# A feed-forward layer with routed experts, twice around an attention layer: both passes sort in two parts, the late chain stands among the shared tiles, and the routing weights are applied at the mix

## The chip, the cores and the metric

One core of one Trainium2 chip runs the whole program in one launch. The metric is the device time of an execution in microseconds (us); several executions give a median.

## The reference, cut to what matters

```python
def ffn(x):                       # x: (2, 1024, 128); 7 routed experts, top 2, HID = 352
    out = expert(x, sg, su, sd)   # silu(h @ g.T) * (h @ u.T) @ d.T, the shared expert
    probs = softmax(x @ wr.T + rb)
    scores, idx = top_k(probs, 2);  scores = scores / scores.sum(-1)
    w = sum(scores[..., None] * one_hot(idx, 7), axis=-2)
    for e in range(7):
        out = out + w[..., e:e+1] * expert(x, rg[e], ru[e], rd[e])
    return out

x = x + 0.5 * ffn(layernorm(x))
x = x + attention(layernorm(x))   # 16 heads of 8, causal, sequence 1024, batch 2
x = x + 0.5 * ffn(layernorm(x))   # same weights
```

## The kernel before, in words

2048 tokens are 16 tiles of 128 (TT), or 4 chunks of 512 (NCH). Everything is fp32, and each product is made of three fp32r products of high and low halves; so every operand is split on its way, the high half by ACT (a cast) and the low one by DVE (a subtraction). The passes of the feed-forward layer are f = 0 and f = 1.

*Sorting.* Of each token the router (`router_dve`, L510, a chain of 15 small DVE operations and one exp on ACT) finds two experts. `places_pe` (L575) counts with two matmuls, `places_dve` (L631) makes from the counts the row of each (token, choice), and `experts_dve` (L655) which expert each of the NJ = 38 routed tiles has. Then POOL sorts: `sort_pool` (L923) is one indirect DMA that writes 128 rows of 132 numbers (weight, id, 128 values, id, weight) into `z_rows` in DRAM, 32 of them in a pass (L928). As the last tile of an expert isn't full, `z_rows` is blanked before (`blank_sp`, L1038), pass 0's 2.6 MB and pass 1's 9.1 MB, on SP's queue at the start. SP loads the sorted tiles back to `zg` in ten batches (`rows_load_sp`, L960; 2 tiles, then 4 each): pass 0 in one DMA per batch, pass 1, where each expert has a fixed region of rows, one per tile from an address in a register. Pass 0 sorts all tokens in one part (PARTS); pass 1 sorts chunks 0 and 1 and then 2 and 3, but its tiles are listed once, after both.

*The tiles' loop.* `ffn_pe`, `ffn_act` and `ffn_dve` (L769, L819, L907) go through the same steps, one job each: 13 (pass 0) or 14 (pass 1) shared tiles, the 38 routed tiles, the other shared tiles (BEFORE, JOBS, L76). A job is 6 matmuls for gate and up (L707 to L709), silu on ACT (L799), the product on DVE (L840; for a routed tile times the weight of the row, L843), 3 transposes (L723), high and low half (L807, L849), 6 matmuls down (L733, L736), and the way out on DVE: two adds to `x` for a shared tile (L888, L890), one reduction to the ring `ys` of 8 for a routed one (L884), from where POOL scatters it to `y_rows` (`scatter_pool`, L932). Step `BEFORE + j - 2` transposes the batch that begins with routed tile j (L756; `batch_at`). In pass 0 the first 8 steps also carry a weight group each (transposes on PE, halves on ACT and DVE; 24 groups in all, TP_FIRST = 16 of them ahead of the loop). At the end SP loads the two rows of each token back, chunk by chunk, and `mix_dve` (L895) adds them to x (L904).

*Order by hand.* Each engine's list is written out in `build` (L1765). Pass 0: norm and logits of all four chunks, router, places, experts, weights, `ffn`. Pass 1: during the last group of heads the chain of chunks 0 and 1 runs (projection, norm, logits, router); after it TAIL_PE, TAIL_ACT, TAIL_DVE (L1720) do the same for chunks 2 and 3 before `ffn_pe(K, 1)` begins. POOL does all sorts, then all scatters, in order. SP's queue: inputs, blank of pass 0, constants of the attention, blanks of pass 1, sorted tiles, clears of `keys` (L1117, 12 DMAs of 512 KB), loads for the mix, attention.

Of the kernel before, what the change touches and what calls it, by code (L numbers as in the profile page):

```python
# [69 lines left out]
assert sum(n for _, n in BATCHES) == NJ  # L70
# [22 lines left out]
def at_bank(q):  # L93
    return AT_BANKS[q % 2]
# [12 lines left out]
ROW = 2 + EMB + 2  # L107
W_COLS, ID_COLS = (0, ROW - 2), (1, ROW - 1)
# [87 lines left out]
def loads(p, u, d):  # L196
# [12 lines left out]
TP_GROUPS = [("g", 0), ("u", 0), ("g", 1), ("u", 1), ("d", 0), ("d", 1)] + \  # L209
            [(w, x) for x in range(2, EXPERTS) for w in ("g", "u", "d")]  # L210
NTP = len(TP_GROUPS)
TP_FIRST = 16
# [4 lines left out]
PM_BANK = [EARLY_BANKS[0], EARLY_BANKS[1], 3, 4]  # L217
LATE_N_BANK = [EARLY_BANKS[2], EARLY_BANKS[1], 5, 3]
R_BANKS = [[R_BANK], [EARLY_BANKS[0], R_BANK]]
# [4 lines left out]
N_CONST2 = 8  # L224
N_SPARES = 4
N_GIVEN = 4
# [9 lines left out]
def place_memory(K, ctx):  # L236
# [8 lines left out]
    K.z_dram = [K.nc.dram_tensor(f"z_rows{f}", (SORTED[f], ROW), F32, kind="Internal").ap() for f in range(2)]  # L245
# [23 lines left out]
    K.rank_i = sb("rank_i", [P, NGATE], mybir.dt.int32)  # L269
    K.stats = sb("stats", [P, 2, TPC, 6])  # L270
# [3 lines left out]
    K.rstd = sb("rstd", [P, 2, TPC])  # L274
    K.z0 = sb("z0", [P, TPC, EMB])
# [3 lines left out]
    K.ids = sb("ids", [P, 2, TT])  # L279
    K.again = {SPAN: sb("again", [P, NGATE, SPAN]), TT: sb("again_half", [P, NGATE, TT])}  # L280
# [3 lines left out]
    K.d_run = sb("d_run", [P, NGATE * SPAN])  # L284
    K.d_cnt = sb("d_cnt", [P, 7, NGATE])
    K.to_row = sb("to_row", [P, NJ], mybir.dt.int32)
    K.slots = sb("slots", [P, SPAN], mybir.dt.int32)
    K.w_row = sb("w_row", [P, NJ])
    K.id_row = sb("id_row", [P, NJ])
    K.w_at = sb("w_at", [P, NJ], mybir.dt.int32)  # L290
    with ExitStack() as s:
        zt = [sb(f"zt_{part}", [P, TOKENS], F32R, scope=s) for part in ("h", "l")]
        with ExitStack() as s2:
# [25 lines left out]
            with ExitStack() as s3:  # L319
# [6 lines left out]
                with ExitStack() as s4:  # L326
# [12 lines left out]
                    K.d_pos = sb("d_pos", [P, NGATE * SPAN], scope=s4)  # L339
                    K.d_slot = sb("d_slot", [P, SPAN], scope=s4)  # L340
# [9 lines left out]
    zrows = [[rows[:, c * TPC:(c + 1) * TPC, 2:2 + EMB] for c in range(NCH)] for rows in K.zrow]  # L350
# [31 lines left out]
    K.z_sc, K.spares, K.given = sem("z_sc"), sem("spares"), sem("given")  # L382
# [5 lines left out]
    K.consts2 = sem("consts2")  # L388
    K.A = {n: sem(f"a_{n}") for n in
# [36 lines left out]
def norm_rstd_pool(K, k, c):  # L426
    e, v = K.nc.gpsimd, c % 2
    e.wait_ge(K.NS[k]["mv"], c + 1)
    e.tensor_scalar(K.var_e[:, v, :], K.mv[:, v, :, 1], LN_EPS, None, ALU.add).then_inc(K.NS[k]["rstd"], 1)
    e.wait_ge(K.NS[k]["rstd"], 2 * c + 1)  # L430
    e.tensor_tensor(K.rstd[:, v, :], K.var_e[:, v, :], K.half_neg[:, :], ALU.pow).then_inc(K.NS[k]["rstd"], 1)


def norm_z_dve(K, k, c):
    e, v = K.nc.vector, c % 2
    e.wait_ge(K.NS[k]["rstd"], 2 * c + 2)
    e.wait_ge(K.NS[k]["mv"], c + 1)
    if c > 1 and k == 1:
        e.wait_ge(K.NS[k]["tr"], c - 1)
# [28 lines left out]
def part_of(f, c):  # L468

    return next(h for h, (t0, t1) in enumerate(PARTS[f]) if t0 <= c * TPC < t1)  # L470


def logits_pe(K, f, k, c):

    e = K.nc.tensor
    if f == 0 and c == 0:
        e.wait_ge(K.sw_lo, 5)
    e.wait_ge(K.NS[k]["lo"], c + 1)
    if f == 1 and c == 0:
        e.wait_ge(K.A["xup"], 2)  # L480
    for t in range(c * TPC, (c + 1) * TPC):
# [20 lines left out]

def chosen(K, f, h):

    t0, t1 = PARTS[f][h]
    flat = K.r_sel[:, 2 * t0 * NGATE:2 * t1 * NGATE]
    return flat.rearrange("p (r t e) -> p r t e", r=2, e=NGATE)


def router_dve(K, f, h):  # L510
    e, s, (t0, t1) = K.nc.vector, K.RS, PARTS[f][h]
    n, ts = t1 - t0, slice(t0, t1)
    r_log, r_exp, r_c, r_w = (v[:, ts, :] for v in (K.r_log, K.r_exp, K.r_c, K.r_w))
# [5 lines left out]
    if f == 0:  # L519
        e.wait_ge(K.ld["bias"], 16 * N_BIAS)  # L520
# [1422 lines left out]
```

## Time and profile before

| what | us |
|---|---|
| median of 3 runs (lowest to highest) | 751.13 (746.61 to 751.75) |
| the profiled execution, its own time | 749.79 |
| its span, first to last instruction | 747.8 |
| PE busy | 608.3 (81%) |
| DVE busy | 479.6 (64%) |
| ACT busy | 311.4 (42%) |
| POOL busy | 210.0 (28%) |
| mean granted clock of PE | 0.895 of full speed |

The trace is of one execution; its own time stands 2.0 us over its span and 1.3 under the median. PE, DVE, ACT, POOL and SP are the engines (TensorE, VectorE, ScalarE, GpSimd, SyncE); PEld is PE's weight load, which overlaps its matmuls. A busy share is a mean over stages that have different limits, so stages are read one at a time. L12 is line 12 of the kernel.

### The profile page before, as it was taken

How to read it: one execution, taken by the hardware profiler on the slowest of the kernel's cores; microseconds unless marked ns; L12 is line 12 of the kernel's file. 1: busy time of each engine (PE TensorE's matmuls, PEld its weight loads, DVE VectorE, ACT ScalarE, POOL GpSimd, SP SyncE). 2: the span in 40 equal slices, each digit the busy share in tenths (PEclk: the TensorE clock that was granted, in tenths of full speed). 3: DMA queues.
4: the chain of work that ended last, by engine and by line, in shares of the span. 5: the costliest groups of instructions: out<-in, count | busy, mean ns of one | idle time of the engine just before them, and what ended most of it. 6: DMA issues, size and time to landing. Idle time of an engine off the chain costs nothing.

```text
span 747.8 us, 12989 instructions
## 1 busy us (share of the span) xinstructions
PE 608.3 (81%) x3900; PEld 453.4 (61%) x3900; DVE 479.6 (64%) x1178; ACT 311.4 (42%) x628; POOL 210.0 (28%) x284
## 2 busy tenths in 40 slices
PE   3642799999837789999999999999977539999990
PEld 3531788999736445555555555554556438999980
DVE  8730566666684796777777776775456326766663
ACT  2230334444314106566665656566751013344440
POOL 5177003444333101111121112111226730244440
PEclk9985799999956799999999999999985559999996
DMA  9996695000246502112020202000001123101006
GB/s 225 320 370 244 167 211 123 27 31 30 66 120 211 193 3 57 37 24 59 3 58 0 58 0 58 1 1 4 1 2 38 51 62 88 34 25 33 29 29 172
DMA packets 44657, 61.03 MB, mean 82 GB/s; under 512 B 5495, under 2 KB 35198, under 8 KB 43582
## 3 DMA queue, kind: packets, MB, share of 16 engines
q1 hardware_dynamic: 39104, 50.72, 24.3%
q0 software_dynamic: 4480, 9.25, 3.7%
q8 instruction: 29, 0.48, 0.3%
q10 hardware_dynamic: 1022, 0.40, 0.3%
q14 instruction: 22, 0.18, 0.1%
HBM read 29.79 MB, written 30.30 MB: 80 GB/s over the span
## 4 chain that ended last, share of the span: by engine, by line
PE 67%; DVE 9%; issue 6%; another core or an unknown queue 5%; DMA 4%; ACT 3%; POOL 2%; SPq 1%; POOLq 0%; DVEq 0%; ACTq 0%
PE psum L1348 11%; PE psum L1370 10%; PE psum L1305 10%; PE psum L733 6%; PE psum L707 5%; PE psum L709 4%; PE psum L708 4%; PE psum L723 4%; PE psum L736 4%; DVE mxp L1422 3%; PE psum L1310 2%; DMA yc<-y_rows 2%; PE psum L756 2%; ACT probs L1482 1%
## 5 line engine op out<-in xcount | busy, mean ns | idle before, releaser
L1422 DVE TENSOR_REDUCE mxp<-psum 128x4 f32<-128x512 f32 x288 | 184.3, 685 | 58.7 <-PE psum L1305 33.0
L1482 ACT ACTIVATE probs<-psum 128x512 f32<-128x512 f32 (+1 forms) x304 | 164.4, 586 | 120.7 <-PE psum L1348 117.3
L1348 PE MATMUL psum<-queries,keys 128*128 128x512 f32 (+3 forms) x384 | 133.2, 395 | 0.5 <-ACT probs L1482 0.2
L1305 PE MATMUL psum<-keys,queries 128*128 128x512 f32 (+3 forms) x384 | 128.2, 381 | 5.1 <-DMA queries<-q_stack 3.0
L935 POOL DMA_INDIRECT y_rows<-ys,to_row x76 | 72.8, 958 | 176.6 <-DVE ys L884 173.8
L799 ACT ACTIVATE silu<-psum 128x352 f32<-128x352 f32 x108 | 50.1, 464 | 142.9 <-PE psum L709 111.0
L1533 POOL TENSOR_SCALAR_AFFINE_SELECT probs<-probs 128x512 f32<-128x512 f32 x64 | 40.6, 635 | 210.4 <-ACT probs L1482 210.4
L1305 PEld LDWEIGHTS psum<-keys,queries 128*128 128x128 f32 x384 | 70.4, 195 | 41.1 <-DVE mxp L1422 32.9
L1348 PEld LDWEIGHTS psum<-queries,keys 128*128 128x128 f32 x384 | 65.6, 190 | 42.6 <-ACT probs L1482 38.1
L733 PE MATMUL psum<-wall,at_h 128*128 (+1 forms) x324 | 69.4, 325 | 21.1 <-DVEq L892 17.8
L1370 PE MATMUL psum<-probs,vg 128*32 128x512 f32 (+3 forms) x768 | 81.8, 498 | 4.8 <-POOL probs L1533 4.8
L723 PE MATMUL psum<-ident,act 128*128 128x128 f32 x324 | 56.3, 285 | 28.6 <-issue 28.3
L843 DVE SCALAR_TENSOR_TENSOR act<-silu,w_row,psum 128x352 f32<-128x352 f32 x76 | 44.1, 581 | 44.2 <-ACT silu L799 33.1
L849 DVE TENSOR_TENSOR at_l<-psum,at_h 128x384 fp32r<-128x384 f32 x108 | 59.6, 552 | 18.3 <-issue 11.6
L733 PEld LDWEIGHTS psum<-wall,at_h 128*128 128x128 f32 x324 | 48.8, 199 | 27.8 <-issue 15.2
L723 PEld LDWEIGHTS psum<-ident,act 128*128 128x128 f32 x324 | 43.4, 146 | 33.1 <-issue 30.3
L807 ACT CAST at_h<-psum 128x384 fp32r<-128x384 f32 x108 | 51.3, 475 | 25.6 <-PE psum L723 11.4
L707 PE MATMUL psum<-wall,zs_h 128*128 x152 | 54.1, 356 | 3.3 <-DVE zs_l L871 3.3
L736 PE MATMUL psum<-wall,at_l 128*128 (+1 forms) x324 | 50.2, 265 | 0.0
L709 PE MATMUL psum<-wall,zs_l 128*128 x152 | 49.4, 325 | 0.0
L708 PE MATMUL psum<-wall,zs_h 128*128 x152 | 49.3, 324 | 0.0
L736 PEld LDWEIGHTS psum<-wall,at_l 128*128 128x128 f32 x324 | 47.8, 199 | 0.0
(221 smaller groups left out, 881.2 us busy)
## 6 DMA issues: line engine op xcount, KB each, us to landing
z_rows<-zg SPq DMA_DIRECT2D x4, 2508.0 KB, 14.1
keys<-q_stack SPq DMA_DIRECT2D x12, 512.0 KB
yc<-y_rows SPq DMA_DIRECT2D x16, 256.0 KB, 3.5
keys<-k_stack SPq DMA_DIRECT2D x32, 128.0 KB, 4.3
queries<-q_stack SPq DMA_DIRECT2D x8, 512.0 KB, 4.2
zg<-z_rows SPq DMA_DIRECT2D x38, 66.0 KB, 1.8
zg<-z_rows SPq DMA_DIRECT2D x9, 264.0 KB, 4.7
k_stack<-zt_h SPq DMA_DIRECT2D x8, 256.0 KB, 3.1
```

What stands on the lines that cost most here:

```text
L707: e.matmul(dst, zh, weight(K, base, hi, HID), start=True, stop=False)
L708: e.matmul(dst, zh, weight(K, base, lo, HID), start=False, stop=False)
L709: ins = e.matmul(dst, zl, weight(K, base, hi, HID), start=False, stop=True)
L723: ins = e.transpose(bank(K, at_bank(q))[:, k * P:(k + 1) * P], K.act[:, q % 2, k * P:(k + 1) * P], K.ident[:, :])
L733: e.matmul(dst[:, 0:2 * EMB], K.at_h[:, q % 2, k * P:(k + 1) * P], weight(K, base, DN + 2 * k * EMB, 2 * EMB), start=(k == 0), stop=False, ...
L736: ins = e.matmul(dst[:, 0:EMB], K.at_l[:, q % 2, k * P:(k + 1) * P], weight(K, base, DN + 2 * k * EMB, EMB), start=False, stop=(k == 2), s ...
L935: e.indirect_dma_start(K.y_dram[f], bass.IndirectOffsetOnAxis(ap=K.to_row[:, j:j + 1], axis=0), K.ys[:, j % RING_Y, :], None).then_inc(K.y ...
L1305: ins = e.matmul(dst[:, at0 * P:(at0 + nb) * P], K.queries[u][:, i * P:(i + 1) * P], K.keys[u][:, j, k0 * P:(k0 + nb) * P], start=(m == 0) ...
L1348: ins = e.matmul(slot(K, u, d, n)[:, m * (q1 - q0):(m + 1) * (q1 - q0)], K.keys[v][:, j, kt * P:(kt + 1) * P], K.queries[v][:, q0:q1], sta ...
L1370: ins = e.matmul(bank(K, O_BANK[half])[32 * j:32 * j + 32, q0 - half * CHUNK:CHUNK], K.vg[:, kt, j, :], K.probs[:, kt % 2, j, q0:q1], star ...
L1422: e.tensor_reduce(K.mxp[:, j, 4 * b:4 * b + 4], bank(K, r_bank).rearrange("p (m k) -> p m k", k=P), AX.X, ALU.max).then_inc(K.A["taken"], 1)
L1482: e.activation(K.probs[:, kt % 2, heads[0]:heads[-1] + 1, q0:q1], src, ACT.Exp, scale=SCALE).then_inc(K.A["ex"], 1)
```

## The change

- Both passes sort in two parts (chunks 0 and 1, chunks 2 and 3), into fixed regions of REGION = 2176 rows per expert. No region is blanked in pass 0: seven more indirect DMAs (`pads_pool`) write 128 rows of zeros behind each expert's last row, and only six tiles at the end (EXTRA) are blanked. Pass 1's rows (8.3 MB, now 130 numbers each) are blanked behind pass 0's loads and the clears.
- The list of routed tiles has two parts (`lists_dve`): ten tiles (WHOLE) that part 0 alone fills, in whole tiles, then the other 28. SP loads each list when its part is sorted, in both passes one DMA per tile.
- Behind every indirect DMA of a sort and of the first ten scatters POOL clears 384 numbers of `idle` (`pause_pool`).
- The row carries id and a code of the first choice, no weight. DVE finds from the code whether a row is a first or second choice (`rows_ids_dve`); the weights are kept in `K.w` and applied in `mix_dve`, one 128x128 operation per tile and choice.
- The normalised values come from ACT (`norm_z_act`), except for chunks 0 and 1 of the last norm; POOL makes two more small operations per chunk for it.
- Pass 0: only 11 weight groups stand ahead of the loop; part 1's router, places and both lists stand in its steps 0 to 5. Pass 1: the late chain of chunks 2 and 3 stands in steps 0 to 11 of the loop.
- A shared tile's and expert's weights are read from a static place, not through a register. `act` is transposed into one bank, not two, until step 13 or 16.

```diff
+HALF = TT // 2
+PARTS = [(0, HALF), (HALF, TT)]
+WHOLE = -(-(SEQ * 2 - ROUTED * (P - 1)) // P)
+LISTS = [(0, WHOLE), (WHOLE, NJ - WHOLE)]
+REGION = TOKENS + P
...
-TP_FIRST = 16
+TP_FIRST = 11
...
+def norm_z_act(K, k, c):
+    e, v = K.nc.scalar, c % 2
+    e.wait_ge(K.NS[k]["rstd"], 4 * c + 4)
...
+    for t in range(TPC):
+        ins = e.activation(K.z[k][c][:, t, :], K.x[:, c * TPC + t, :], ACT.Identity, bias=K.mr_neg[:, v, t:t + 1],
+                           scale=K.rstd[:, v, t:t + 1])
+    ins.then_inc(K.NS[k]["z"], 1)
...
+def lists_dve(K, f, h):
...
+    e.tensor_tensor(ends, tile0.unsqueeze(2).to_broadcast(wide), cnt(K, ENDS, ROUTED).unsqueeze(1).to_broadcast(wide),
+                    ALU.is_ge).then_inc(s["at"], 1)
+    e.wait_ge(s["at"], routed(f, h, "at", 1))
+    e.tensor_reduce(raw[:, 0, :], ends, AX.X, ALU.add).then_inc(s["at"], 1)
...
@@ act_tr_pe
     if q >= 2:
-        e.wait_ge(s["lo"], q - 1)
-    if q == 1:
-        e.wait_ge(K.RS["slot"], routed(f, len(PARTS[f]) - 1, "slot", 1))
+        e.wait_ge(s["lo"], q - 1 if q > ONE_AT[f] else q)
+    elif q:
+        e.wait_ge(s["lo"], q)
...
@@ ffn_pe
+        for what, c in (FRONT_PE if f == 0 else TAIL_PE).get(step, ()):
+            late_pe(K, f, what, c)
...
@@ act_dve
-    kind, n = JOBS[f][q]
-    if kind == "s":
-        e.tensor_tensor(act, silu, up, ALU.mult).then_inc(s["act"], 1)
-    else:
-        e.wait_ge(s["ids"], 3 * BATCH_OF[n] + 3)
-        e.scalar_tensor_tensor(act, silu, K.w_row[:, n:n + 1], up, ALU.mult, ALU.mult).then_inc(s["act"], 1)
+    e.tensor_tensor(act, silu, up, ALU.mult).then_inc(s["act"], 1)
...
@@ mix_dve
-        e.tensor_tensor(x, x, K.yc[:, c % 2, r, :, :], ALU.add).then_inc(s["mix"], 1)
+        for t in range(TPC):
+            x = K.x[:, c * TPC + t, :]
+            ins = e.scalar_tensor_tensor(x, K.yc[:, c % 2, r, t, :], K.w[:, r, c * TPC + t:c * TPC + t + 1], x,
+                                         ALU.mult, ALU.add)
+        ins.then_inc(s["mix"], 1)
...
+PAUSE = 3 * P
...
+def pads_pool(K):
+    e = K.nc.gpsimd
+    e.wait_ge(K.RS["cnt"], routed(0, 1, "cnt", 4))
+    for x in range(ROUTED):
+        e.indirect_dma_start(K.z_dram[0], bass.IndirectOffsetOnAxis(ap=K.pad_at[:, x:x + 1], axis=0),
+                             K.zero[:, :], None).then_inc(K.z_sc[1], 16)
+        pause_pool(K)
+
+def pause_pool(K):
+    rested_pool(K)
+    K.nc.gpsimd.memset(K.idle[:, :], 0.0).then_inc(K.rested, 1)
+    K.rests += 1
...
@@ rows_load_sp
     for b, (j0, n) in enumerate(BATCHES):
...
+        if j0 in (0, WHOLE):
+            h = 0 if b == 0 else 1
+            e.wait_ge(K.z_sc[h], sorts(f, h))
         for j, row in zip(range(j0, j0 + n), rows):
-            e.dma_start(K.zg[:, j, :], K.z_dram[1][at(row, P), :]).then_inc(K.z_ld[b], 16)
+            e.dma_start(K.zg[:, j, :], K.z_dram[f][at(row, P), :]).then_inc(K.z_ld[b], 16)
...
+FRONT_PE = {3: (("places", 1),)}
+FRONT_DVE = {0: (("router", 1),), 2: (("lists", 0),), 4: (("places", 1),), 5: (("lists", 1),)}
+TAIL_PE = {1: (("proj_tr", 2), ("proj_tr", 3)), 2: (("proj", 2),), 3: (("proj", 3),), 5: (("norm_tr", 2),),
+           6: (("norm_tr", 3),), 8: (("logits", 2), ("logits", 3)), 11: (("places", 1),)}
+TAIL_ACT = {0: (("gather", 2), ("gather", 3)), 1: (("proj", 2), ("proj", 3)), 4: (("z", 2),),
+            5: (("z", 3), ("norm_hi", 2)), 6: (("norm_hi", 3),), 9: (("router", 1),)}
+TAIL_DVE = {0: (("places", 0),), 1: (("proj_lo", 2), ("proj_lo", 3)), 2: (("x", 2), ("stats", 2)),
+            3: (("x", 3), ("stats", 3)), 4: (("lists", 0),), 6: (("norm_lo", 2),), 7: (("norm_lo", 3),),
+            9: (("router", 1),), 11: (("places", 1), ("lists", 1))}
...
@@ build
             clear_sp(K)
+            blank_sp(K, 1, SORTED // P)
             ffn_sp(K, 0)
...
             attn_pe(K)
-            for step, c in TAIL_PE:
-                late_pe(K, step, c)
             ffn_pe(K, 1)
...
             sort_part_pool(K, 0, 0)
+            sort_part_pool(K, 0, 1)
+            pads_pool(K)
             scatters_pool(K, 0)
```

## Rows read from the trace of the kernel before

**Rows 1.** The page's strip of 40 slices of 18.7 us, in tenths.

```profile
PE   3642799999837789999999999999977539999990
...
PEclk9985799999956799999999999999985559999996
```

**Rows 2.** Stages: stretch, length, busy us (instructions), clock, DMA share, GB/s.

```profile
60.00:70.00 10.00, 1.67 (x6) 1.21 (x5) 0.00 (x0) 0.00 (x0) 7.57 (x8) 0.50 0.77 275
...
90.00:120.00 30.00, 28.07 (x195) 26.55 (x194) 21.09 (x59) 12.18 (x29) 2.07 (x3) 0.94 0.97 205
...
575.00:585.00 10.00, 3.38 (x12) 2.64 (x11) 8.56 (x33) 2.47 (x4) 7.79 (x8) 0.50 0.16 54
...
600.00:610.00 10.00, 0.90 (x3) 0.50 (x3) 1.44 (x4) 1.26 (x3) 4.79 (x5) 0.50 0.18 54
...
640.00:680.00 40.00, 38.00 (x278) 36.36 (x277) 28.37 (x70) 16.63 (x38) 15.33 (x16) 1.00 0.09 28
```

**Rows 3.** Timeline, first hole: start, us, engine, operation, idle before it.

```profile
61.17 0.49 PE L709 MATMUL psum<-wall,zt_l 128*128 128x352 f32 x1
...
71.93 0.46 ACT L799 ACTIVATE silu<-psum 128x352 f32<-128x352 f32 x1 [13.54 <-remote]
```

**Rows 4.** Timelines round the sorts; last, tile `z_rows` (ns min/median/max).

```profile
4.84 0.30 POOL L1091 MEMSET again<- 128x256 f32 x1
...
33.13 1.23 POOL L928 DMA_INDIRECT z_rows<-zrow,slots  x1 [16.90 <-DMA z_rows<-zg]
...
78.24 0.48 ACT L807 CAST at_h<-psum 128x384 fp32r<-128x384 f32 x1 [5.85 <-remote]
...
565.76 1.10 POOL L928 DMA_INDIRECT z_rows<-zrow_late,slots  x1 [0.20 <-issue]
...
L928 POOL DMA_INDIRECT z_rows<-zrow,slots x32: 954/958/1232, 33.1 to 72.5; - x32
```

**Rows 5.** Chain that ended last: batches from routed tiles 10, 34, 10.

```profile
125.00 0.63 PE psum L756 x4
...
181.06 0.63 PE psum L756 x4
...
653.74 0.63 PE psum L756 x4
```

**Rows 6.** Groups by line: xcount, busy us, mean ns, idle before.

```profile
L849 DVE TENSOR_TENSOR at_l<-psum,at_h 128x384 fp32r<-128x384 f32 x108 | 59.6, 552 | 18.3 <-issue 11.6 <-ACT at_h L807 6.3
...
L840 DVE TENSOR_TENSOR act<-silu,psum 128x352 f32<-128x352 f32 x32 | 16.6, 520 | 44.4 <-issue 31.0 <-ACT silu L799 13.0 <-DVE x L890 0.2
...
L888 DVE TENSOR_TENSOR x<-x,psum 128x128 f32<-128x128 f32 x32 | 9.0, 280 | 7.3 <-remote 3.6 <-PE psum L736 3.5
...
L1198 DVE TENSOR_TENSOR wall<-psum,wall 128x352 fp32r<-128x352 f32 x16 | 7.9, 517 | 5.4 <-issue 3.6 <-ACT wall L1179 1.4 <-DVE x L890 0.3
```

**Rows 7.** Timeline, pass 1: router, table load, router's end, last count.

```profile
574.23 0.23 DVE L523 TENSOR_TENSOR r_log<-psum,rb_row 128x64 f32<-128x64 f32 x1 [1.96 <-PE psum L486]
...
575.53 1.28 ACT L799 ACT_TABLE_LOAD   x1
...
578.10 0.18 DVE L559 TENSOR_TENSOR zrow_late<-r_p,zrow_late 128x8 f32<-128x8 f32 x1
...
583.56 0.24 DVE L675 TENSOR_SCALAR w_at<-d_raw 128x38 int32<-128x38 f32 x1
```

**Rows 8.** Timeline, pass 0: router begins; weight transposes begin.

```profile
22.81 0.29 DVE L523 TENSOR_TENSOR r_log<-psum,rb_row 128x128 f32<-128x128 f32 x1 [2.03 <-PE psum L486]
...
28.02 0.77 PE L1150 MATMUL psum<-ident,nat_g 128*128 128x128 f32 x3
```

**Rows 9.** Timeline: the attention's last transposes on PE.

```profile
554.63 0.62 PE L1333 MATMUL psum<-ident,ot 128*128 128x128 f32 x4
```

**Rows 10.** Timeline: SP's first loads of sorted tiles in pass 1.

```profile
607.71 17.00 SPq L979 DMA_DIRECT2D zg<-z_rows  x22
```

**Rows 11.** Groups by line: the adds of the mix.

```profile
L904 DVE TENSOR_TENSOR x<-x,yc 128x512 f32<-128x512 f32 x16 | 11.0, 686 | 9.6 <-DMA yc<-y_rows 9.3
```

More of the change, by code:

```diff
@@ L349, in place_memory @@
         K.zrow[1] = sb("zrow_late", [P, TT, ROW], scope=s)
-    zrows = [[rows[:, c * TPC:(c + 1) * TPC, 2:2 + EMB] for c in range(NCH)] for rows in K.zrow]
+    zrows = [[rows[:, c * TPC:(c + 1) * TPC, 0:EMB] for c in range(NCH)] for rows in K.zrow]
     K.z = [zrows[0], [K.z0[:, :, :], z1[:, :, :]] * 2, zrows[1]]
@@ L468, in part_of @@
 def part_of(f, c):
-    return next(h for h, (t0, t1) in enumerate(PARTS[f]) if t0 <= c * TPC < t1)
+    return next(h for h, (t0, t1) in enumerate(PARTS) if t0 <= c * TPC < t1)
 def logits_pe(K, f, k, c):
@@ L480, in logits_pe @@
         e.wait_ge(K.A["xup"], 2)
+    if f == 1 and c == 2:
+        e.wait_ge(K.NS[k]["lo"], NCH)
+    if f == 0 and c == 2:
+        e.wait_ge(K.RS["slot"], routed(0, 0, "slot", 1))
     for t in range(c * TPC, (c + 1) * TPC):
@@ L678, in experts_known @@
-def experts_known(f):
-    return (f + 1) * ROUTE_STEPS["at"]
+    total = run[:, :, TT - 1]
+    if h == 0:
+        e.tensor_copy(cnt(K, FIRST_HALF), total).then_inc(s["cnt"], 1)
+        e.tensor_tensor(cnt(K, FIRST_AT), total, K.region[:, :], ALU.add).then_inc(s["cnt"], 1)
+        slots_dve(K, f, h, run, K.region[:, :])
+    else:
+        slots_dve(K, f, h, run, cnt(K, FIRST_AT))
+        e.tensor_tensor(cnt(K, TOTAL), total, cnt(K, FIRST_HALF), ALU.add).then_inc(s["cnt"], 1)
+        e.wait_ge(s["cnt"], routed(f, h, "cnt", 2))
+        if f == 0:
+            e.tensor_tensor(cnt(K, PADS), cnt(K, TOTAL), K.region[:, :], ALU.add).then_inc(s["cnt"], 1)
+            e.wait_ge(s["cnt"], routed(f, h, "cnt", 3))
+            e.tensor_scalar(K.pad_at[:, :], cnt(K, PADS, ROUTED), K.lane[:, 0:1], None, ALU.add).then_inc(s["cnt"], 1)
+        else:
+            e.sem_inc(s["cnt"], 2)
@@ L787, in ffn_pe @@
             up_pe(K, f, step, bases[step])
-        if f == 1 and step == 1:
-            places_pe(K, f, 1)
         if 0 <= step - 1 < NQ:
@@ L822, in ffn_act @@
             weights_hi_act(K, TP_FIRST + step)
+        for what, c in TAIL_ACT.get(step, ()) if f == 1 else ():
+            late_act(K, what, c)
         b = batch_at(f, step)
@@ L903, in mix_dve @@
             e.wait_ge(s["mix"], 2 * c + 1)
-        e.tensor_tensor(x, x, K.yc[:, c % 2, r, :, :], ALU.add).then_inc(s["mix"], 1)
+        for t in range(TPC):
[3 more added lines that the diff above has]
+        ins.then_inc(s["mix"], 1)
 def ffn_dve(K, f):
     for step in range(NQ + 2):
+        for what, c in (FRONT_DVE if f == 0 else TAIL_DVE).get(step, ()):
+            late_dve(K, f, what, c)
         if f == 0 and TP_FIRST + step < NTP:
@@ L1105, in ids_pool @@
 def ids_pool(K, f, h):
[L1107 to L1109 removed]
+    t0, t1 = PARTS[h]
+    K.nc.gpsimd.tensor_copy(K.zrow[f][:, t0:t1, ID], K.ids[:, t0:t1]).then_inc(K.numbered, 1)
 def pad_pool(K, f):
@@ L1760, in late_dve @@
         norm_z_dve(K, 2, c)
+    elif step == "norm_lo":
+        norm_lo_dve(K, 2, c)
+    elif step == "router":
+        router_dve(K, f, c)
+    elif step == "places":
+        places_dve(K, f, c)
     else:
-        norm_lo_dve(K, 2, c)
+        lists_dve(K, f, c)
 def build(nc, tokens, attn_w, attn_b, proj_w, proj_b, gate_s, up_s, down_s, gate_r, up_r, down_r,
@@ L1844, in _ @@
             attn_act(K)
-            for step, c in TAIL_ACT:
-                late_act(K, step, c)
             ffn_act(K, 1)
```

459 lines of the change are left out of this document (242 added, 217 removed).

## The prediction

> **What bounds the kernel now.** I read the 40-slice strip first. The reader is to see two holes in the PE row, slices 3 to 4 and 30 to 32, both also at half clock [rows 1]; between them lies the attention, which the change leaves as it is. The table of stages gives their depth: of 60 to 70 us PE is busy 1.67 us, DVE and ACT nothing, and POOL 7.57 us; of 600 to 610 us PE 0.90 us and POOL 4.79. The DMA share is 0.77 in one and 0.18 in the other, so full DMA engines aren't what both have in common; POOL at work in indirect DMAs is. In a stretch where POOL issues one such DMA per tile, 16 in 40 us, PE runs 38.0 of 40 us [rows 2].
>
> The timeline of the hole shows what waits: PE ended the up projection at 61.66 us (61.17 + 0.49), and the silu that needs nothing else ran at 71.93, with the releaser "remote" [rows 3]. In this time POOL issues the 32 sort DMAs of pass 0 without a break, 33.1 to 72.5 us, 0.96 us each and 0.30 us apart, a pitch of 1.26. ACT's next operation comes at 78.24 us, after the last of them, though its input (the transposes right behind 71.93's silu) had long been there [rows 4]. My reading, an inference: each indirect DMA also costs something that semaphores or sequencers of the others share; it drains in (78.24 - 33.13) / 32 = 1.41 us and is fed every 1.26. A backlog grows through the sort and the other engines are held, once it is long, until it has drained.
>
> So both feed-forward passes lose their shared tiles, which were to cover the sort. The sort ends at 73.5 us and the step that brings in routed tile 10 (step 21 of the job list, third batch of four) starts at 125.0 us; its twin in the second pass (step 22) at 653.74. From there on a routed tile takes (181.06 - 125.00) / 24 = 2.34 us and PE is the bound [rows 5]. The change can move those two points; what lies behind them keeps its length.
>
> **Pass 0.** Two things set the new step 21: when the engines get there (A) and when the second list can be loaded (B).
>
> A. The weights' transposes began at 28.02 us, when the last load had landed [rows 8]; that stays. Eleven groups instead of 16 stand ahead of the tiles; two are done early and nine take 7 us at the 0.77 us of three transposes [rows 8]: step 0 at about 36 us. A shared step with a weight group costs DVE 0.52 + 0.55 + 2 x 0.28 + 0.52 = 2.15 us plus gaps, 2.3 us, and PE at full clock no more [rows 6]. DVE is thus the bound, and what the change adds to DVE there counts in full: the router of half the tiles takes 578.28 - 574.23 = 4.1 us; from its end over places and list to the last count 583.80 - 578.28 = 5.5 us, which I split by the number of operations into 2.2 for places and 3.3 for the list [rows 7]. Part 1's router, its places and two lists lie among the steps: 4.1 + 2.2 + 0.6 (pads' three small operations) + 2 x 3.3 = 13.5 us, bounds 11 and 16, since the first list is 10 wide and not 38 and the second has one operation more. 36 + 13 x 2.3 + 13.5 = 79.5, with the table load 80.5 us; eight steps of 2.3 and one dip of the clock, 20 us: step 21 at 101.
>
> B. Half the router starts early: it needs chunks 0 and 1 only, and DVE has lost the normalisation (to ACT) and two thirds of the small weights ahead of it. Before, the full router started at 22.81 [rows 8] and the sort at 33.13, where POOL had waited 16.9 us, its last releaser the blank of the sort's memory [rows 4]; the blank is now six tiles and no longer waited for by the sort. I put the first router at 16 us and slots at 22.5 (4.1 + 2.5, rows 7). A sort now has a pause behind it: a memset of 384 elements, between the 0.30 us of 256 and 1.5 times that, 0.41; and the DMA after another POOL operation takes 1.10 us after 0.20. Pitch 1.10 + 0.41 + 0.20 = 1.71, I take 1.74; bounds 0.96 + 0.30 + 0.30 = 1.56 and 1.23 + 0.30 + 0.45 = 1.98 [rows 4]. All lie above 1.41, so by my reading nothing piles up. Part 0: 22.5 + 16 x 1.74 = 50 us. Part 1's slots come in step 4: 36 + 4.1 + 4 x 2.3 + 3.3 + 2.2 = 55. With the seven pad DMAs 23 x 1.74 = 40: last issue at 95, landed 97. SP loads one tile per DMA, 17.0 / 22 = 0.77 us each [rows 10]: four and a landing, 101.5 us. A and B meet; step 21 at 102 instead of 125.0: **-23 us** (bounds from pitch and lists -27 and -16). POOL works in order, so routed tile 8 also waits for y buffer 0, whose scatter stands behind the sort: 95 + 3 us, no later than B. The first ten scatters are paused too and run off a backlog of eight at 1.74 us against tiles at 2.34: no cost; at 1.98 still none.
>
> **Pass 1.** Now ffn_pe starts where the attention's last transposes end, 555.3 us [rows 9]; before, the late chain stood here, its logits done at 574.2 [rows 7]. DVE again bounds the steps: 14 x 1.75 (no weight group) = 24.5; late chain without the normalisation, six 128x512 operations of 0.69 [rows 11] and two statistics like four 128x128 operations each, 0.28 and a little [rows 6], 6.6; router 4.1, places 2.5 + 2.2, lists 6.6: 46.5 us. ACT must load tables twice more, since the exp of the router now stands between two silus, 2 x 1.28 [rows 7]; part of it shows, 2 us; waits along the chain I put at 4 us. Step 14 at 555.5 + 52.5 = 608, step 22 at 608 + 19.5 = 627.5. Part 1's places stand at step 11, about 598 us; 16 x 1.74 = 28 gives 626, landed 628, loaded 632. B wins: 632 instead of 653.7, **-22 us** (bounds -26 and -14).
>
> **The rest.** The weights move from the routed tile's product to the mix. DVE's product goes from 0.58 to 0.52 us in 76 tiles, but PE bounds those: nothing. A chunk's mix was two 128x512 adds of 0.69 us [rows 11]; it becomes eight 128x128 operations like the 0.28 us of rows 6: 2.2 against 1.4, +0.8 each. In the end two chunks show: +1.6 us. Between pass 0 and the attention DVE gains 4 x 4 x 0.28 of normalisation and pays 4 x 0.8; ACT and two more POOL operations in the first chain take back about a microsecond: 0, bounds -3 and +3. The tile's weights come from static slices instead of registers for shared tiles: PE has no idle there, nothing. Blanking of pass 1's memory moves from the start (hidden then) to behind the clears on SP's queue. SP ends its loads at 97 + 28 x 0.77 + 2 = 120; the clears are 6.3 MB at the 205 GB/s of their stretch, 30 us; the blank is 8.3 MB in rows of 520 B, at that rate 40 us and done by 190, at the 275 / 0.77 = 357 GB/s of 60 to 70 us 23 and done by 173 [rows 2]. The mix's loads stand behind it, due at 181: between 0 and +9; I take 0, as the stretch of 60 to 70 us was one of blanks, which this is too.
>
> **Sum**, against the profiled execution's 749.8 us: -23 - 22 + 1.6 = 706.4. That execution is 1.3 us under the median of the runs; set against the median the forecast is 707 us.
>
> A rule speaks against more DVE work beside the sort. The Trainium skill (SBUF — State Buffer, "SBUF: two separate sides") says that descriptors of a DMA issued by GpSimd can't be written while DVE runs an operation that takes the port pair they share. By it the sorts would stretch under the copies that now lie beside them. Against it the 32 sorts of pass 0 keep a median of 0.958 and a maximum of 1.232 us [rows 4].
>
> **Rivals.**
> 1. *The pause doesn't help (slower).* If not the pitch but the mere presence of a sort DMA holds the others, the longer sort holds them longer. It decides from the point where a sort at pitch 1.74 lets fewer than half the steps through. Pass 0: part 1 lasts 55 to 95 us, held to 99; the old hole let about two steps pass, so seven of 13 remain: 99 + 16 = 115, step 21 at 135, +10. Pass 1: part 0 holds the late chain to 590, part 1 runs 605 to 633, five steps remain: step 14 at 648, step 22 at 667, +13. With the mix 750 + 25 = 775 us. For: POOL is at sorts all through both holes. Against: from 575 to 585 us POOL was busy 7.79 us with sorts and DVE worked 8.56 all the same, and one scatter per tile never holds anybody [rows 2]. Chance 0.10.
> 2. *Half clock.* [...] A step's 2 us of PE become 3.6 or so; 13 steps and the router's 4: 87 instead of 80.5, +6; in pass 1 14 x 3.5 + 18 us of late chain = 67 against 52.5, of which +9 shows behind B. 722 us. Chance 0.22.
> 3. *The second list's gate.* Pitch at 1.98: 23 x 0.24 = 5.5 and 16 x 0.24 = 4, or the blank in front of the mix's loads, +9: 716 to 725. The Trainium skill (DMA: Bandwidth & Descriptors, "Queues, rings and completion order") has each DMA engine take turns between queues, which would keep the scatters moving beside the blank; it says nothing for SP's own loads behind it. Chance 0.12.
> 4. *More than forecast*: the added DVE work falls into waits and the sort runs at 1.56: 695 us. Chance 0.12.
>
> The forecast as worked out has 0.44 (700 to 714 alone). What a measurement of this kernel can tell from no change is about 1%. Faster by over 1%: all but rival 1 and a tail of 2 and 3, 0.88; within 1% 0.03; slower 0.09. The range reaches from 692 to 738: rivals 2 to 4 with their spread lie in it, rival 1 and mixtures of it with 2 don't.
>
> **What would show it.** PE's row without the two holes; sorts at 1.7 us and no "remote" silu of 10 us; part 0's first sort near 22 us; fourth batch transposed near 102 and 632 us; the routed pitch unchanged at 2.34; adds of the mix eightfold at 0.28. The forecast is wrong if silus still wait many us beside sorts (rival 1), if the granted clock is 0.5 through the shared steps (2), or if the loads of list 1 or of the mix start late (3).

## The result and the profile after

| | before | after |
|---|---|---|
| median, us (range, runs) | 750.33 (746.61 to 751.75, 4) | 721.64 (719.24 to 723.56, 4) |
| profiled execution, us | 749.79 | 723.56 |
| its span, us | 747.8 | 721.8 |
| mean granted clock | 0.895 | 0.921 |

The ratio is 0.962, with a 95% interval of 0.958 to 0.967: faster by 29 us, where 43 were forecast (707 us). The time lies within the range given, 692 to 738.

The page's strip of the changed kernel, 40 slices of 18.0 us:

```profile
PE   3767899998017889999999999999898887999980
...
PEclk9999999999556798999999999999998998999995
DMA  9912148999955701020201020100000011330015
```

The two holes of [rows 1] are gone: slices 3 to 4 now read 67 in PE's row, and in the second pass none falls below 7 before the mix at the end. But there is a new hole, slices 11 and 12 (0 and 1), at 180 to 216 us, where the kernel before had full work. The DMA row stands at 9 in front of it. Two of the stages of [rows 2] in the same view of the kernel after, and the new hole (stretch, length, busy us of PE, PEld, DVE, ACT and POOL, clock, DMA share, GB/s):

```profile
60.00:70.00 10.00, 9.71 (x63) 9.60 (x64) 7.80 (x20) 4.50 (x10) 9.01 (x13) 0.83 0.19 55
70.00:80.00 10.00, 8.44 (x67) 8.11 (x65) 8.57 (x25) 5.11 (x12) 8.93 (x14) 1.00 0.12 41
...
180.00:190.00 10.00, 0.00 (x0) 0.00 (x0) 0.00 (x0) 0.00 (x0) 0.00 (x0) 0.52 1.23 165
```

From 60 to 70 us POOL is busier than before (9.01 against 7.57) and PE works 9.71 us in place of 1.67. From 180 to 190 us no engine does anything, and the DMA share is 1.23 while only 165 GB/s are moved.

The sort and its pause (timeline of POOL), and what answers to [rows 5], the fourth batch in each pass (timeline of PE):

```profile
30.87 0.43 POOL L1016 MEMSET idle<- 128x384 bf16 x1
31.47 0.97 POOL L998 DMA_INDIRECT z_rows<-zrow,slots  x1 [0.17 <-issue]
...
100.51 0.63 PE L819 MATMUL psum<-ident,zg 128*128 128x128 f32 x4 [0.67 <-issue]
...
625.86 0.63 PE L819 MATMUL psum<-ident,zg 128*128 128x128 f32 x4 [0.57 <-issue]
```

And what stands in the new hole: SP's timeline, then DVE's first addition of the mix, then the blank in the list of DMA issues (size, us to landing):

```profile
112.39 7.01 SPq L1218 DMA_DIRECT2D keys<-q_stack  x12
119.44 0.61 SPq L1134 DMA_DIRECT2D z_rows<-zero  x1
183.36 26.86 SPq L1089 DMA_DIRECT2D yc<-y_rows  x8
...
203.45 1.79 DVE L969 SCALAR_TENSOR_TENSOR x<-yc,w,x 128x128 f32<-128x128 f32 x6 [24.14 <-DMA yc<-y_rows]
...
z_rows<-zero SPq DMA_DIRECT2D x1, 8125.0 KB, 82.8
```

Read from the bottom: the blank of pass 1's sorted memory was issued at 119.4 and landed at 202.2 (119.44 + 82.8). DVE had nothing to do from 179.3, and added its first y at 203.5, one microsecond behind the blank. In front of its first load SP also waited 61.2 us for the scatters to land, until 183.4; the last one had been issued at 173.9, so it took 9.5 us, where the last one of pass 0 in the kernel before took 2.2.

With three marks in each trace the time can be laid out piece by piece: the fourth batch of pass 0, the first sort DMA of pass 1, and the fourth batch of pass 1 (starts, from the timelines):

| span of the profiled run | to batch, pass 0 | to first sort, pass 1 | to batch, pass 1 | to the end |
|---|---|---|---|---|
| before: 747.8 | 125.00 | 434.1 | 94.6 | 94.1 |
| after: 721.8 | 100.51 | 454.8 | 70.5 | 95.9 |
| difference: -26.0 | -24.5 | +20.7 | -24.1 | +1.8 |
| forecast: -43.4 | -23 | 0 | -22 | +1.6 |

Three columns came as forecast; in the other one a term that was put at 0 cost 20.7 us. The experiments ask two things: what in the blank costs it, and whether the two gains come from what I gave as their reason.

### The profile page after: what moved, and what is told of

Read it like the earlier page. It is cut to its first block and busy times, and to the rows that moved or that the text cites. A ratio compares the mean times of both kernels' runs of the same rounds, so it can differ in the third digit from the quotient of the medians.

```text
span 721.8 us, 13331 instructions
## 1 busy us (share of the span) xinstructions
PE 597.8 (83%) x3902; PEld 448.2 (62%) x3902; DVE 479.6 (66%) x1244; ACT 330.2 (46%) x671; POOL 259.6 (36%) x402
## 5 line engine op out<-in xcount | busy, mean ns | idle before, releaser
L1402 PE MATMUL psum<-keys,queries 128*128 128x512 f32 (+3 forms) x384 | 130.0, 386 | 4.4 <-DMA queries<-q_stack 2.5
L903 DVE TENSOR_TENSOR act<-silu,psum 128x352 f32<-128x352 f32 x108 | 56.2, 521 | 62.4 <-ACT silu L862 43.3
## 6 DMA issues: line engine op xcount, KB each, us to landing
z_rows<-zero SPq DMA_DIRECT2D x1, 8125.0 KB, 82.8
```

The costliest lines, as they stand in the source:

```text
L1402: ins = e.matmul(dst[:, at0 * P:(at0 + nb) * P], K.queries[u][:, i * P:(i + 1) * P], K.keys[u][:, j, k0 * P:(k0 + nb) * P], start=(m == 0) ...
```

## The experiments

Each is a kernel of its own, compared with the kernel before on the same chip. The medians of before were 749.3, 751.7 and 751.1 us in the three sets, so kernels of different sets are best compared by their ratios.

### A blank in large pieces

From here on this is the kernel that the later edits start from.

```diff
-            blank_sp(K, 1, SORTED // P)
+            blank_wide_sp(K)
...
+def blank_wide_sp(K):
+    e = K.nc.sync
+    e.wait_ge(K.cleared, 16 * 3 * P // (GROUPS * 4))
+    cols = SORTED // P * ROW // 5
+    rows = K.z_dram[1].rearrange("(p b a) c -> p b (a c)", p=P, b=5)
+    src = K.keys[1][:, :, :].rearrange("p j t -> p (j t)")[:, 0:cols].bitcast(F32)
+    e.dma_start(rows, src.unsqueeze(1).to_broadcast([P, 5, cols])).then_inc(K.blank_rows[1], 16)
```

> The changed kernel with one edit: the blank of pass 1's sorted rows keeps its place on SP's queue and its 8.3 MB, but is copied from keys1 (zero once the clears have landed, for which SP now waits) in pieces of 13,000 bytes and no longer from a 520 byte row. Theory (size of the pieces): the blank falls from 82.8 us to some 30, the mix's loads are no longer held, the first mix starts at 180 to 184 us instead of 203.5, and the kernel takes 698 to 703 us. Rival (bytes or place): 8.3 MB behind 6.3 MB of clears take about as long whatever the pieces are; the first mix stays later than 195 us and the kernel above 712. Second rival (the hole only hid another wait, the second hand-over being next): mix at 182 but the attention starts less than 10 us earlier, 710 to 715.

701.98 us (701.55 to 704.19), ratio 0.936 (0.935 to 0.938). That is the theory's number, and this kernel beats both. Its windows, of the kind of [rows 2], and the first addition:

```profile
150.00:160.00 10.00, 7.06 (x49) 6.80 (x48) 5.05 (x13) 2.95 (x7) 3.84 (x4) 0.94 0.98 395
160.00:170.00 10.00, 10.00 (x71) 9.90 (x69) 5.83 (x13) 4.29 (x10) 3.67 (x4) 0.89 1.02 414
170.00:180.00 10.00, 9.27 (x69) 8.69 (x67) 6.86 (x17) 3.82 (x9) 4.01 (x5) 1.00 0.15 49
...
183.70 2.31 DVE L969 SCALAR_TENSOR_TENSOR x<-yc,w,x 128x128 f32<-128x128 f32 x8 [0.89 <-DMA yc<-y_rows]
```

SP issued the blank at 147.7, once the clears had landed. It moved at 395 to 414 GB/s and was over before 180 us. The mix began at 183.7 and not at 203.5, and all of that reached the end: 721.8 - 702.3 = 19.5 us of span. The wide blank isn't free either. While it runs, the batches of pass 0 start at 146.23 and 157.90 us, 11.7 apart, where the others of this stretch are 9.2 apart:

```profile
157.90 0.63 PE L819 MATMUL psum<-ident,zg 128*128 128x128 f32 x4 [2.94 <-issue]
```

What PE waited for there the trace doesn't say. In the change, with its narrow blank, the same two batches are 9.24 us apart.

### The narrow blank from ACT's queue

```diff
@@ def ffn_act(K, f):
+        if f == 0 and step == 26:
+            blank_sp(K, 1, SORTED // P)
@@ def blank_sp(K, f, tiles):
-    K.nc.sync.dma_start(rows, K.zero[:, :].unsqueeze(1).to_broadcast([P, tiles, ROW])).then_inc(K.blank_rows[f], 16)
+    e = K.nc.scalar if f else K.nc.sync
+    e.dma_start(rows, K.zero[:, :].unsqueeze(1).to_broadcast([P, tiles, ROW])).then_inc(K.blank_rows[f], 16)
@@ SP's program
-            blank_sp(K, 1, SORTED // P)
```

> The changed kernel with the blank unchanged in shape (520 byte pieces) but issued from ACT in step 26 of pass 0, near 113 us, so that it is no longer in front of the mix's loads on SP's queue. Theory A (the queue's order costs): the blank still takes 80 us or more, but the mix's loads overtake it; first mix at 182 to 190 us, 700 to 709 us in all. Theory B (the DMA engines are full of small pieces, whoever issues them): the mix's loads crawl too, 10 us or more to landing; first mix at 193 to 203, 712 to 722 us. A third way: ACT itself is held while it issues so many pieces; then its silus show a gap of many us near 113 and the kernel is slower than 722.

717.79 us, ratio 0.958 (0.955 to 0.961), against 0.962 for the change: theory B, in its middle. The edit is made to the changed kernel itself. The windows and the first addition:

```profile
180.00:190.00 10.00, 0.47 (x5) 0.33 (x3) 0.57 (x2) 0.00 (x0) 0.00 (x0) 0.55 1.25 160
190.00:200.00 10.00, 0.00 (x0) 0.00 (x0) 0.00 (x0) 0.00 (x0) 0.00 (x0) 0.50 1.18 184
...
200.27 2.32 DVE L971 SCALAR_TENSOR_TENSOR x<-yc,w,x 128x128 f32<-128x128 f32 x8 [19.15 <-DMA yc<-y_rows]
```

Nothing stands in front of the mix's loads on SP's queue here, and they still come at 200.3 in place of 203.5. The blank took 88.7 us. Its place in the queue is worth about 3 us; the rest is that the DMA engines are busy with it, for the loads (the first ones took 12.8 to 14.5 us to land, where the median of this kernel is 3.8) and for the scatters that the loads wait for (SP's first load was issued at 185.2).

### Small pieces again, from spread places

```diff
-    cols = SORTED // P * ROW // 5
-    rows = K.z_dram[1].rearrange("(p b a) c -> p b (a c)", p=P, b=5)
-    src = K.keys[1][:, :, :].rearrange("p j t -> p (j t)")[:, 0:cols].bitcast(F32)
-    e.dma_start(rows, src.unsqueeze(1).to_broadcast([P, 5, cols])).then_inc(K.blank_rows[1], 16)
+    rows = K.z_dram[1].rearrange("(p b a) c -> p b a c", p=P, b=5)
+    src = K.keys[1][:, :, :].rearrange("p j t -> p (j t)")[:, 0:25 * 160].rearrange("p (a t) -> p a t", t=160)
+    src = src[:, :, 0:ROW].bitcast(F32)
+    for b in range(5):
+        e.dma_start(rows[:, b], src).then_inc(K.blank_rows[1], 16)
```

> The kernel of the wide blank with its blank cut into pieces of 520 bytes again, but read from 25 different places of keys1 (stride 640 bytes) and in five DMAs, still behind the wait for the clears. Theory (the size of a piece costs, 82.8 us / 1000 pieces per DMA engine = 83 ns each): the blank takes 70 to 85 us from about 150, the mix's loads stand behind it, 735 to 750 us, worse than the change since the start is later too. Rival (reading one and the same row of the source over and over was the cost): 25 to 35 us, 700 to 706 us.

724.46 us, ratio 0.964 (0.960 to 0.968). The rival is out: with other source rows the small pieces are as slow. Whether it is reading or writing in small pieces that costs isn't told apart; here both are small.

```profile
150.00:160.00 10.00, 9.25 (x71) 8.94 (x70) 6.92 (x17) 4.24 (x10) 3.94 (x5) 1.00 1.25 166
160.00:170.00 10.00, 10.00 (x75) 9.72 (x74) 6.64 (x16) 4.03 (x11) 3.83 (x4) 1.00 1.22 187
...
208.24 2.05 DVE L969 SCALAR_TENSOR_TENSOR x<-yc,w,x 128x128 f32<-128x128 f32 x7 [26.71 <-DMA yc<-y_rows]
```

But my size was off too. The five DMAs were issued from 148.4 on and were over by 208, so under 60 us, not 70 to 85. I had counted the 82.8 us as the blank's own; in the change it was issued behind twelve clears, and in the wide kernel these alone held the queue until 147.7. I estimate its own time at some 54 us (148 to 202): 8.32 MB at 154 GB/s, against 395 to 414 GB/s in the wide blank. The change's own windows agree: 238 GB/s from 143 to 146 us, the clears, and 185 from 146 to 149.

### The pauses alone, in the kernel before

```diff
                         K.zrow[f][:, t, cols], None).then_inc(K.z_sc, 16)
+    pause_pool(K)
+
+
+def pause_pool(K):
+
+    if K.rests:
+        K.nc.gpsimd.wait_ge(K.rested, K.rests)
+    K.nc.gpsimd.memset(K.nat_wide[:, :].bitcast(BF16), 0.0).then_inc(K.rested, 1)
+    K.rests += 1
```

nat_wide is the memory of nat_route with 32 columns more, free once the router's weights are transposed.

> The kernel before with one edit: behind each of its 32 sort DMAs of either pass a memset of 320 elements and a wait for it, so the pitch goes from 1.26 to about 1.5 us, above the 1.41 at which I think they drain. Theory (backlog): no silu waits 10 us any more; the shared tiles run beside the sort, step 21 near 107 us instead of 125.0 and step 22 of pass 1 near 640 instead of 653.7; 712 to 725 us in all. Rival (the mere presence of sort DMAs holds the others): the holes stay and last 8 us longer each; 755 to 770 us.

720.16 us (717.66 to 722.64), ratio 0.962 (0.958 to 0.966): as much as the whole change. The stage that was the first hole of [rows 2], and its part of the second:

```profile
60.00:70.00 10.00, 9.58 (x68) 8.92 (x67) 7.26 (x20) 3.86 (x9) 8.84 (x15) 1.00 0.59 215
...
575.00:585.00 10.00, 10.00 (x64) 9.73 (x64) 6.21 (x16) 3.44 (x8) 8.84 (x15) 0.84 0.13 42
```

PE works 9.58 us of 60 to 70 with the same 32 sorts beside it, which end later (the last is issued at 80.2 and not at 72.5 us). The fourth batch came at 106.69 us (107 expected) and in pass 1 at 622.28. The rival, that the presence of sort DMAs holds the others, is refuted by one memset per DMA.

### The changed kernel's structure without pauses

```diff
 def pause_pool(K):
-    rested_pool(K)
-    K.nc.gpsimd.memset(K.idle[:, :], 0.0).then_inc(K.rested, 1)
-    K.rests += 1
+    pass
```

> The kernel of the wide blank with all pauses taken out: sorts at a pitch of 1.26 us, but still in parts of 16 (and 16 with seven pads). By the backlog theory a backlog grows by 0.15 us per sort and the first hole of the kernel before opened after 22 sorts, so part 0 stays under it and part 1 with its pads just reaches it: silus wait at most 2 to 5 us at the end of part 1, the lists come 5 us or more earlier, and the time is within 4 us of the wide blank's, either way. If instead any unpaused sort holds the others, both parts do: holes of 5 us or more in each part, and 10 to 20 us slower. If the split alone did it, no hole at all and 0 to 6 us faster.

749.50 us (747.21 to 752.43), ratio 1.0005 (0.999 to 1.002): all 47 us of the wide kernel's gain are gone. None of the three expectations had this size; "any unpaused sort holds the others" is nearest. The fourth batch of pass 0 comes at 124.86 us, where the kernel before had 125.00, with half the sort done early, five weight groups fewer ahead of the tiles and the rest of the change in place. ACT's timeline beside part 1, whose DMAs run from 59.0 to 87.7 us at a pitch of 1.26:

```profile
68.93 0.48 ACT L870 CAST at_h<-psum 128x384 fp32r<-128x384 f32 x1 [0.96 <-PE psum L786]
75.99 0.45 ACT L1280 CAST wall<-psum 128x352 fp32r<-128x352 f32 x1 [6.58 <-remote]
85.12 0.46 ACT L862 ACTIVATE silu<-psum 128x352 f32<-128x352 f32 x1 [8.68 <-issue]
90.75 0.48 ACT L870 CAST at_h<-psum 128x384 fp32r<-128x384 f32 x1 [5.17 <-remote]
```

From 68.9 to 90.8 us ACT does three operations; the waits between them, 6.6, 8.7 and 5.2 us, are put down to no engine, and they end 3 us behind the last DMA. In pass 1's part 1 it is the same: a silu at 631.6 waited 9.5 us, the DMAs having run from 609.1 to 629.0.

### How long a pause

```diff
-PAUSE = 3 * P
+TILE, PAUSE = 3 * P, 2 * P
...
-    K.nc.gpsimd.memset(K.idle[:, :], 0.0).then_inc(K.rested, 1)
+    K.nc.gpsimd.memset(K.idle[:, 0:PAUSE], 0.0).then_inc(K.rested, 1)
```

The others have P, 4 * P and 5 * P; the two longer ones clear a larger `idle`.

> The kernel of the wide blank with a shorter pause, a memset of 256 elements in place of 384: pitch 0.97 + 0.30 + 0.17 = 1.44 us. In the kernel without pauses the last DMA of a part was followed by the end of its hold after 1.32 to 1.42 us per sort, so a sort drains in about 1.4 us, and 1.44 is still above it. Theory (a drain rate of 1.4): no holds, sorts 1.5 to 3 us shorter per part, engines rather than lists decide: 699 to 703 us. Rival (the room that a pause gives must be much larger, or the wait for the DMA's descriptor is what helps and not the rate): holds of 3 us or more return, 705 to 725.

> As before with a memset of 128 elements, pitch 0.97 + 0.2 + 0.17 = 1.34 us, below 1.4. Theory (rate): a backlog grows by 0.06 us a sort, less than half of the 0.14 without pauses, so part 0 shows none or a short hold and part 1 with its pads one of a few us: 702 to 720 us. Rival (any small operation with a wait between two sorts is enough, whatever its length): no hold, 698 to 702. Rival (all or nothing below the rate): 735 to 750, as without pauses.

> The kernel of the wide blank with a longer pause, a memset of 512 elements: pitch 0.97 + 0.54 + 0.17 = 1.68 us. Pauses of 0, 128, 256 and 384 elements gave 749.5, 740.1, 719.6 and 702.0 us, and at 384 silus in the shared tiles still waited 13.9 us in all on no engine (issue), half of it in each pass's part 1. Theory (what is held shrinks steadily with the pitch, and the rest of it is still on the path): 694 to 700 us. Rival (the lists' gate: at 384 the engines and the second list meet already, and 23 sorts of 0.11 us more make the list 2.5 us later in either pass): 702 to 707. Rival (nothing is left to win and the gate has that much slack): 701 to 703.

> The same with 640 elements, pitch 1.79 us. By either theory the lists' gate rules here: the last DMA of pass 0's sort is issued at 63.5 + 23 x 1.79 = 97 (55.7 + 41.2) us, loads follow to 104, and part 1 of pass 1 ends 5 us later than at 384; step 21 at 104 to 106 and step 22 at 611 to 613: 706 to 712 us. If holds were still the larger cost it would be below 702.

| elements | memset, us | pitch, us | median, us (range) | ratio | batch, pass 0 | first sort to batch, pass 1 |
|---|---|---|---|---|---|---|
| none | - | 1.26 | 749.50 (747.2 to 752.4) | 1.000 | 124.9 | 87.8 |
| 128 | 0.218 | 1.35 | 740.12 (738.8 to 743.8) | 0.986 | 121.7 | 82.8 |
| 256 | 0.325 | 1.46 | 719.55 (712.6 to 721.0) | 0.958 | 109.5 | 72.7 |
| 384 | 0.433 | 1.57 | 701.98 (701.6 to 704.2) | 0.936 | 100.2 | 70.7 |
| 512 | 0.538 | 1.67 | 703.89 (702.5 to 707.7) | 0.936 | 101.4 | 72.3 |
| 640 | 0.645 | 1.78 | 709.75 (705.6 to 711.6) | 0.945 | 101.6 | 70.5 |

The memset rows from which the pitch is made (0.96 or 0.97 for the DMA and 0.17 between) look like this, for 256 (ns min/median/max):

```profile
L1016 POOL MEMSET idle<- x91: 325/325/337, 28.0 to 630.4; 128x256 bf16 x91
```

A rate of 1.4 us, above which all is well, is refuted: 1.46 us still costs 16 to 18 us more than 1.57 (by the ratios and by the medians). Neither is a small operation with a wait enough, whatever its length, nor is it all or nothing: up to 384 elements the time falls from step to step with the pitch. 384 and 512 are equal within their intervals (0.935 to 0.938, 0.933 to 0.938), and 640 is slower than either.

At 384 elements silus still waited 20.6 us in all with the releaser "issue", at 512 7.0 and at 640 5.0. That no longer shortens the kernel, since the longer sort takes back what the engines win: the last pad of pass 0 is issued at 90.7, 92.4 and 94.9 us, and in pass 1 the fourth batch, which waits for nobody in the wide kernel (384), waits for the loads of the second list with 512 and with 640:

```profile
607.68 0.63 PE L819 MATMUL psum<-ident,zg 128*128 128x128 f32 x4 [0.63 <-issue]
```

```profile
608.29 1.02 PE L819 MATMUL psum<-ident,zg 128*128 128x128 f32 x4 [1.96 <-DMA zg<-z_rows]
```

```profile
608.85 0.63 PE L819 MATMUL psum<-ident,zg 128*128 128x128 f32 x4 [3.00 <-DMA zg<-z_rows]
```

In pass 0 it doesn't wait for them in any of the three. The columns of the table are of single executions: those profiled for 256 and 640 were shorter than their medians (716.2 and 705.6 us), those for 384 and 512 longer (704.2 and 707.7). So of the 8 us that 640 loses against 384, 3.0 are seen as a wait; where its median loses the rest, the trace doesn't tell.

### The late chain ahead of the tiles again

```diff
-TAIL_PE = {1: (("proj_tr", 2), ("proj_tr", 3)), 2: (("proj", 2),), 3: (("proj", 3),), 5: (("norm_tr", 2),),
-           6: (("norm_tr", 3),), 8: (("logits", 2), ("logits", 3)), 11: (("places", 1),)}
+TAIL_PE = {0: (("proj_tr", 2), ("proj_tr", 3), ("proj", 2), ("proj", 3), ("norm_tr", 2), ("norm_tr", 3),
+               ("logits", 2), ("logits", 3)), 2: (("places", 1),)}
```

TAIL_ACT and TAIL_DVE are changed alike: all of the chain up to the router in step 0, the lists of part 0 in step 1, the places of part 1 in step 2 and its list in step 3.

> The kernel of the wide blank with one part of the change undone: in pass 1 the late chain (second half's projection, normalisation and router) stands ahead of the shared tiles again, places of part 1 at step 2 instead of 11. Theory (DVE work among tiles is cheaper than a chain alone): the chain alone takes about 23 us with PE mostly idle, among tiles it cost about 13 of DVE; step 22 moves from 607.7 to 616 to 620 and the kernel takes 710 to 715 us. Rival (the second list's gate decided in the wide blank's kernel, where its last sort was issued at 600.6 and the batch transposed at 607.7): the earlier places bring the list forward by 10 us and give the loss back; within 3 us of 702.

712.35 us (711.55 to 713.13), ratio 0.948 (0.945 to 0.951), so the chain's place is worth 1.2%, 9 us (0.948 against 0.936): the theory. Its windows show what a chain alone looks like, PE at half clock:

```profile
535.00:545.00 10.00, 6.39 (x29) 5.80 (x27) 5.66 (x22) 2.69 (x6) 6.12 (x11) 0.50 0.04 13
545.00:555.00 10.00, 5.72 (x25) 4.95 (x25) 1.38 (x2) 2.83 (x7) 8.82 (x16) 0.50 0.10 33
```

The second list was ready some 9 us earlier than in the wide kernel (last sort DMA at 591.4, not 600.6), and the fourth batch came 8 us later (615.26, not 607.68). So in these kernels it is the engines that set the batch, and the chain alone makes them later. The wide kernel's list has little to spare, though: its loads began at 603.1 us, 4.6 before the batch, and with 512 elements, where the last sort DMA came 0.9 us later, the batch waited (above).

## Why the prediction was right, and where it was wrong

**The reading of the holes: right in kind, wrong in its number.** "Each indirect DMA also costs something that semaphores or sequencers of the others share" holds as far as this: the pause alone gives 29 us in the kernel before, and without it the rest of the change, wide blank included, leaves the time where it was. What is shared is not shown. Rival 1, the slower one, is thereby out. But the rate "drains in 1.41 us" was worked out from one end of one hole, and as a threshold it is false; had the pause been 256 elements, every pitch above 1.41 and "by my reading nothing piles up", the kernel would have been 16 to 18 us slower than with 384. That the two gains came out as forecast is in part luck: the change happened to stand at 1.57. The pitch itself I had put at 1.74, bounds 1.56 and 1.98; 0.97 + 0.43 + 0.17 = 1.57 is the lower one. I had given the DMA behind a pause the 1.10 us of one row of [rows 4], which stood behind another kind of operation; behind a memset the median is 0.967. (A slip in reading the strip: counted from 1, the second hole is slices 31 to 33, not 30 to 32.)

**Pass 0, -23: right** (-24.5). Step 21 forecast at 102 came at 100.5. The first sort came at 26.4 and not 22.5, and the shorter pitch made up for it: the last pad was issued at 89.5 and not at 95. **Pass 1, -22: right** (-24.1). But I had B, the loading of the second list, as what decides, at 632 against 627.5 for the engines. The sort ended 7 us earlier than I had it (last DMA 618.9, not 626), and the batch came at 625.9 without a wait for the loads (its 0.57 us are put down to "issue"): A decided. **The mix, +1.6: right** (+1.8): eight operations in 2.32 us against 1.42.

**The step that failed** is the last of "the rest": the blank in front of the mix's loads, "between 0 and +9; I take 0, as the stretch of 60 to 70 us was one of blanks, which this is too". It cost 20 us, more than the 17.4 that the forecast was short of, since the two gains were 3.6 us larger than forecast. The rate for it was read in a stretch where a blank ran, but the blank of the kernel before was made of 20 KB pieces from zg and the new one of 520 byte rows from zero; both were known from the two kernels. My own slower bound took 205 GB/s, the clears' own stretch; the blank ran at 154 by the estimate above. Clears until 148 and 54 us of blank make 202, where the mix's loads were due at 181: +21. The same step also named the wrong place: I had only SP's queue in mind, but on ACT's queue the same blank costs 16.6 of its 19.8 us (first addition at 200.3 and 203.5, against 183.7), since loads and scatters go slowly beside it whatever queue it is on. The Trainium skill (DMA: Bandwidth & Descriptors, "Queues, rings and completion order"), as cited in the prediction, has the DMA engines take turns between queues. This trace agrees in kind, as the scatters did go on landing, though the last took 9.5 us and not 2.2; taking turns kept them moving and did not keep them fast. By the other rule cited there, that of the Trainium skill (SBUF — State Buffer, "SBUF: two separate sides") on the port pair that DVE and GpSimd share, the sorts would have stretched. Their median went from 0.958 to 0.967 us beside a DVE that is 78 to 86% busy, so no run here shows it; which of DVE's operations take that pair wasn't looked at.

**The rivals.** Half clock (722, 0.22) gives the right total for a wrong reason: the granted clock is 0.83 to 1.00 in the shared steps of pass 0 and 0.69 to 1.00 in those of pass 1, and both passes came out as short as forecast. The second list's gate (716 to 725, 0.12) holds the measured 721.6 and has the right term, the blank ahead of the mix's loads, but at 9 us in place of 20. Its other half, the gate at the sort, did nothing. The sort ran at 1.57 us as in rival 4 (1.56, 695 us), and the kernel whose blank is wide came to 702.0.

**What gave what**, from the same marks in the traces. Without pauses the new structure gives nothing in pass 0 (125.0 and 124.9 for the first mark, in two very different kernels). In pass 1 it gives 6.8 us of the profiled run (87.8 against 94.6), of which 4.4 are lost again in the other two columns, and the medians are equal. With pauses and the old structure the marks are 106.7 / 437.0 / 78.6 / 93.4, with the new structure and the wide blank 100.2 / 436.9 / 70.7 / 94.6. In pass 0 the new structure is 6.5 us ahead, but the two have different pitches, 1.51 and 1.57 us, and at 1.46 the new structure has 109.5, later than the old one's 106.7; so how much of the 6.5 is due to the two-part sort isn't shown. In pass 1 it is 8 us ahead, and the kernel with the chain in front, at the same pitch as the wide one, has 79.0 in that column: all 8 go with the place of the late chain.

What stays open is what it is that a close row of indirect DMAs holds. The runs show that what it costs grows as the pitch falls from 1.57 to 1.26 us, that it begins within ten or so DMAs, that it ends 2 to 3 us behind the last one, and that the profile puts the waits down to no engine. No run tells apart the semaphore path from the sequencers, nor whether the number of elements in each DMA matters.

## What to carry to other kernels

Before pricing a DMA by the rate of another stretch, compare the pieces of the two: the same 8.3 MB took 54 us in 520 byte rows and about 25 us in 13 KB ones (24.5 to landing where the profile has it, in the kernel without pauses), and the small ones slowed the scatters and the mix's loads, from either queue. Where POOL issues indirect DMAs in a row and the other engines show waits for nobody, try a pause behind each before moving work about, in several lengths: here one memset per DMA in the old kernel gave as much as the whole change (720.2 and 721.6 us), and without it the rest of the change gave nothing in all. A threshold worked out from one event is a guess, and a forecast that stands on which side of it a number lies should carry the slope on the other side in its range.

## What had not been expected of the hardware

- A memset of 0.43 us between indirect DMAs of GpSimd, which makes GpSimd's own sort a quarter slower, takes 47 us off the kernel that has the rest of the change (749.5 to 702.0 us); one of 0.22 us takes about 10.
- 16,000 rows of 520 bytes keep the DMA share at 1.2 with 150 to 190 GB/s moved; 640 pieces of 13 KB move 395 to 414 GB/s at a share of 0.98 to 1.02.
- The profile doesn't put these waits on GpSimd: the silus of the kernel before waited 31.2 us for "remote", 13.5 at most, and the products on DVE behind them 31.0 for "issue".
